# Token places computed by GpSimd at the start of the second attention instead of by VectorE at the end of the stage before it

## The reference, cut to what matters

```python
xn = _layernorm(x)
x = x + _L1_attn_ref(xn, ...) + _L1_ffn_ref(xn, ...)      # layer 1
# in _L1_ffn_ref:
scores = sigmoid(xf @ gate_w + bias)                       # (4096, 8)
top_scores, top_idx = top_k(scores, 2)
top_scores = top_scores / (sum(top_scores) + 1e-06)
w = zeros((T, E)).at[arange(T)[:, None], top_idx].add(top_scores)
...
combined = einsum('teh,te->th', eo * 0.1, w)
```

## Time and profile before

| | us |
|---|---|
| median of 3 runs | 1206.17 |
| lowest, highest | 1204.74, 1207.23 |
| the profiled execution | 1203.1 |
| its span, first to last instruction | 1201.4 |

### The profile page before, as it was taken

How to read it: one execution, slowest core, us unless ns; L and a number is a source line. 1 busy time by engine, 2 the same in 40 slices (tenths; PEclk the granted TensorE clock), 3 DMA queues, 4 the chain that set the end, 5 groups by cost and what they waited for, 6 DMA issues and landing times. The chain is left out here.

```text
span 1201.4 us, 22310 instructions
## 1 busy us (share of the span) xinstructions
PE 1078.3 (90%) x7591; PEld 595.4 (50%) x7598; DVE 930.1 (77%) x1984; ACT 724.4 (60%) x1110; POOL 471.8 (39%) x809
## 2 busy tenths in 40 slices
PE   4767878999999999999999886999999879999997
PEld 2335664333334344333334464444444358888874
DVE  7979997878888888888887353788878546777776
ACT  3647641466666666666666553466666657778761
POOL 7101221133323333332554320476776712566630
PEclk9988997799999999999999887699999989999999
DMA  5322592011211222122101022222222263677452
GB/s 141 97 89 65 113 147 31 19 54 55 72 63 56 82 72 74 55 84 71 57 5 35 1 78 83 66 62 67 68 62 68 68 198 120 200 243 243 157 133 78
DMA packets 99953, 106.10 MB, mean 88 GB/s; under 512 B 21505, under 2 KB 77334, under 8 KB 99776
## 3 DMA queue, kind: packets, MB, share of 16 engines
q1 hardware_dynamic: 93904, 95.65, 29.8%
q0 software_dynamic: 4992, 8.48, 2.1%
q10 hardware_dynamic: 944, 0.54, 0.2%
HBM read 65.20 MB, written 38.45 MB: 86 GB/s over the span
## 5 line engine op out<-in xcount | busy, mean ns | idle before, releaser
L1256 ACT ACTIVATE a_probs<-a_pst 128x1024 f32<-128x1024 f32 (+4 forms) x544 | 411.9, 808 | 206.8 <-PE a_pst L1200 199.4
L1279 DVE TENSOR_REDUCE a_tops<-a_ps 128x1 f32<-128x512 f32 (+9 forms) x624 | 338.2, 589 | 71.1 <-PE a_ps L1154 68.8
L1098 POOL TENSOR_SCALAR_AFFINE_SELECT a_probs<-a_probs 128x256 f32<-128x256 f32 (+3 forms) x384 | 180.2, 481 | 331.2 <-ACT a_probs L1256 326.8
L1154 PE MATMUL a_ps<-kp,qp 96*128 96x256 bf16 (+10 forms) x2112 | 291.0, 253 | 8.8 <-PEq L1407 4.5
L1200 PE MATMUL a_pst<-qp,kp 98*128 98x512 bf16 (+4 forms) x1088 | 260.8, 332 | 17.7 <-ACT a_probs L1256 12.7
L1154 PEld LDWEIGHTS a_ps<-kp,qp 96*128 96x128 bf16 (+1 forms) x2112 | 140.2, 99 | 214.2 <-DVE a_tops L1279 100.9
L1219 PE MATMUL a_po<-a_probs,vh 128*32 128x512 f32 (+4 forms) x2176 | 229.6, 498 | 12.1 <-POOL a_probs L1098 11.3
L1279 DVE TENSOR_REDUCE a_tops_lead<-a_ps 128x1 f32<-128x512 f32 x256 | 165.1, 685 | 19.1 <-PE a_ps L1154 18.3
L1200 PEld LDWEIGHTS a_pst<-qp,kp 98*128 98x128 bf16 (+1 forms) x1088 | 83.4, 99 | 113.5 <-ACT a_probs L1256 64.8
L1911 POOL DMA_INDIRECT chosen_rows<-e_slot_y,e_slot_x x92 | 93.3, 1014 | 96.9 <-DVE e_slot_y L2131 75.1
L2119 DVE TENSOR_TENSOR e_tails<-e_hidden,e_heads 128x512 fp32r<-128x512 f32 x124 | 86.0, 694 | 39.8 <-ACT e_heads L2053 37.6
(11 more groups left out here) (330 smaller groups left out, 1513.2 us busy)
## 6 DMA issues: line engine op xcount, KB each, us to landing
e_slot_w<-weight_parts SPq DMA_DIRECT2D x23, 1024.0 KB
qp<-q_parts SPq DMA_DIRECT2D x64, 96.0 KB
slot_rows<-empty_row SPq DMA_DIRECT2D x4, 1495.0 KB, 26.6
e_slot_x<-slot_rows SPq DMA_DIRECT2D x23, 260.0 KB, 3.2
a_raw<-in_wraw SPq DMA_DIRECT2D x18, 256.0 KB, 3.9
weight_parts<-first_rows SPq DMA_DIRECT2D x9, 512.0 KB, 4.4
weight_parts<-a_cut SPq DMA_DIRECT2D x9, 512.0 KB, 3.0
qp<-q_parts SPq DMA_DIRECT2D x64, 64.0 KB
```

What stands on the lines that cost most here:

```text
L1098: pool.affine_select(out=seen, in_=seen, compare_op=ALU.is_ge, fill=0.0, base=m0, pattern=[[0, 2], [1, mw]], channel_multiplier=-1 if laye ...
L1154: last = pe.matmul(bank[:, i * room + at:i * room + to], sb["qp"][slot][0:rows, j, f["qt"] * P:(f["qt"] + 1) * P], sb["kp"][slot][0:rows, ...
L1256: act.activation(probs[local % RING][0:st["rows"], 2 * part:2 * part + 2, st["off"]:CHUNK], p_st[part][0:st["rows"], :, st["off"]:CHUNK], ...
L1279: dve.tensor_reduce(out, scores, AX.X, ALU.max).then_inc(s["banks_read"], 1)
```

## The change

VectorE keeps three instructions at the end of `between_layers`: the totals are rounded as before, now into a tensor `counted` that stays, and the 256 columns of ranks are copied out of PSUM into a new tensor `ranks`. The rest is computed by GpSimd in the block of attention 1, behind `stage(0)` and `stage(1)` and before its first mask. GpSimd's version adds in three halving steps where VectorE had one `tensor_reduce`, and makes `passed_by` in eight instructions. Temporary tensors move from one block's memory to the other's.

```diff
@@ between_layers, VectorE
-            def place_tokens():
...
+            def copy_ranks():
+
                 dve.wait_ge(plan["ranked"], START + 1)
...
+                dve.tensor_scalar(sb["counted"][:, :], p_y[:, TILES * EXPERTS:(TILES + 1) * EXPERTS], float(CHUNK - 1), None, ALU.add)\
+                    .then_inc(plan["plan_steps"], 1)
+                dve.tensor_copy(sb["ranks"][:, :], p_y[:, 0:TILES * EXPERTS]).then_inc(plan["plan_steps"], 1)
+                dve.wait_ge(plan["plan_steps"], START + 1)
+                dve.tensor_scalar(sb["counted"][:, :], sb["counted"][:, :], (1 << 31) - CHUNK, None, ALU.bitwise_and)\
+                    .then_inc(plan["plan_steps"], 1)
...
-            place_tokens()
+            copy_ranks()
@@ attention, GpSimd
+            def place_tokens():
+
+                step = plan["plan_steps"]
+                ranks = sb["ranks"][:, :].rearrange("p (t e) -> p t e", e=EXPERTS)
+                narrow = [P, EXPERTS, EXPERTS]
+                pool.wait_ge(step, START + 3)
+                pool.tensor_copy(spread[:, :], sb["counted"][:, :]).then_inc(step, 1)
+                pool.wait_ge(step, START + 4)
+                pool.tensor_tensor(upto[:, :, :], sb["upto"][:, :, :], spread[:, :].unsqueeze(1).broadcast_to(narrow),
+                                   ALU.mult).then_inc(step, 1)
+                for i, half in enumerate((4, 2, 1)):
+                    pool.wait_ge(step, START + 5 + i)
+                    pool.tensor_tensor(upto[:, :, 0:half], upto[:, :, 0:half], upto[:, :, half:2 * half], ALU.add)\
+                        .then_inc(step, 1)
...
+                for i in range(EXPERTS):
+                    pool.tensor_scalar(passed_by[:, :, i], sb["firsts"][:, :], region_ends[:, i:i + 1], 1.0,
+                                       ALU.is_ge, ALU.mult).then_inc(step, 1)
...
+                for i, half in enumerate((4, 2, 1)):
+                    pool.wait_ge(step, START + EXPERTS + 12 + 2 * i)
+                    pool.tensor_tensor(chosen[:, :, :, 0:half], chosen[:, :, :, 0:half], chosen[:, :, :, half:2 * half],
+                                       ALU.add).then_inc(step, 1)
...
             stage(0)
             stage(1)
+            if layer == 1:
+                place_tokens()
             for what, n, k, part in order:
```

More of the change, by code:

```diff
@@ L962, in attention @@
         e = sb["counts"]["experts"]
+        if layer == 1:
+            plan = sb["counts"]["plan"]
+            spread = tmp("spread", [P, EXPERTS])
+            upto, region_base = tmp("upto", [P, EXPERTS, EXPERTS]), tmp("base", [P, EXPERTS])
+            place, chosen = tmp("place", [P, TILES, EXPERTS]), tmp("chosen", [P, TOPK, TILES, EXPERTS])
+            passed_by = tmp("passed_by", [P, SLOT_TILES, EXPERTS])
         if layer == 0:
@@ L1073, in draw_after @@
                                    channel_multiplier=-1).then_inc(drawn, 1)
+            def place_tokens():
[11 more added lines that the diff above has]
+                        .then_inc(step, 1)
+                region_ends = upto[:, :, 0]
+                pool.wait_ge(step, START + 8)
+                pool.tensor_tensor(region_base[:, :], region_ends, spread[:, :], ALU.subtract).then_inc(step, 1)
+                for i in range(EXPERTS):
+                    pool.tensor_scalar(passed_by[:, :, i], sb["firsts"][:, :], region_ends[:, i:i + 1], 1.0,
+                                       ALU.is_ge, ALU.mult).then_inc(step, 1)
+                pool.wait_ge(step, START + 9)
+                pool.tensor_tensor(place[:, :, :], ranks, region_base[:, :].unsqueeze(1).broadcast_to([P, TILES, EXPERTS]),
+                                   ALU.add).then_inc(step, 1)
+                pool.wait_ge(step, START + EXPERTS + 10)
+                for i in range(TOPK):
+                    pool.tensor_tensor(chosen[:, i, :, :], sb["hot"][:, i, :, :], place[:, :, :], ALU.mult).then_inc(step, 1)
+                for i, half in enumerate((4, 2, 1)):
+                    pool.wait_ge(step, START + EXPERTS + 12 + 2 * i)
+                    pool.tensor_tensor(chosen[:, :, :, 0:half], chosen[:, :, :, 0:half], chosen[:, :, :, half:2 * half],
+                                       ALU.add).then_inc(step, 1)
+                    pool.tensor_tensor(passed_by[:, :, 0:half], passed_by[:, :, 0:half], passed_by[:, :, half:2 * half],
+                                       ALU.add).then_inc(step, 1)
+                pool.wait_ge(step, START + EXPERTS + 18)
+                pool.tensor_copy(sb["slots"][:, :, :], chosen[:, :, :, 0]).then_inc(step, 1)
+                pool.tensor_scalar(sb["expert_of"][:, :], passed_by[:, :, 0], 1.0, float(EXPERTS - 1), ALU.mult, ALU.min)\
+                    .then_inc(step, 1)
@@ L1421, in between_layers @@
         den = tmp("den", [P, BT])
[L1422 to L1426, removed]
         p_t, p_y, p_xn, p_c, p_k, p_v = (bank(n) for n in "pt py pxn pc pk pv".split())
@@ L1732, in choose @@
                                   den[:, :].unsqueeze(2).broadcast_to([P, BT, TOPK]), ALU.mult).then_inc(step, 1)
-            def place_tokens():
[L1736 to L1739, removed]
-                dve.wait_ge(plan["ranked"], START + 1)
[L1741 to L1767, removed]
@@ L2206, in build @@
         keep("gates", [P, TILES, TOPK])
+        keep("ranks", [P, TILES * EXPERTS])
+        keep("counted", [P, EXPERTS], I32)
         keep("slots", [P, TOPK, TILES], U32)
```

## The result

| | before | with the change |
|---|---|---|
| median (us) | 1207.23 of 5 | 1200.74 of 5 |
| lowest, highest | 1204.74, 1208.61 | 1200.22, 1202.74 |
| the profiled execution | 1203.1 | 1200.41 |
| its span | 1201.4 | 1198.7 |

The ratio is 0.9956, 95% interval 0.9944 to 0.9968: 5.3 us faster, 3.9 to 6.8. (The kernel before ran again beside the changed one, so its median is now 1207.23. The ratio and its interval are an estimate of their own and not the quotient of the two medians, which differ by 6.5 us.) The forecast was 3.1 us less and 1203.1; the time lies in the range, and the gain is larger than the working gave.

What follows compares the result with a forecast made beforehand. VectorE's list at the end of `between_layers` was taken to hold up every engine: -3.43 us for shortening it and +0.3 for the collision make -3.1, so 1206.17 becomes 1203.1 us, range 1200.0 to 1205.6.

Steps and rivals of the forecast that it cites:

- What bounds the place: End of `between_layers`: every engine waits 4 us for VectorE's list of small instructions; VectorE still reports last after the change.
- The 3.43 us: End of `between_layers`: VectorE's list ends at 744.83 against 748.26, and all of this comes off attention 1's start.
- the rounding: Last of VectorE's three kept instructions, taken to follow the copy of the ranks, 0.17 us.
- TensorE's idle time: Before attention 1: about 1.0 us in place of 4.45, with nothing taken for it in the sum.
- idle time ahead of the experts: Sign of a wrong prediction: the 3.4 us return as idle time of all engines before the experts.
- GpSimd's chain: Start of attention 1: 25 instructions and twelve waits, 8.5 us, costing nothing on the path, 5.3 us to spare.
- The collision: First unit's tail in attention 1: L1293 on VectorE slowed beside GpSimd's chain, 0 to 0.88 us, taken as 0.3 lost.
- The clock: Start of attention 1: rival that TensorE keeps 2.4 GHz, giving 1199.9 us, chance 0.09; expected instead to fall after 5 to 8.
- The rival of a long chain: Start of attention 1: GpSimd's chain delays the masks, 25.5 us giving 1214.5; slower case, chance 0.06.
- The sum: Whole kernel: -3.43 + 0.3 = -3.1 us, taken off the median of 1206.17.
- The case to which the prediction gave 0.66: Whole kernel: the forecast case, 2.4 to 4.5 us faster.

Runs made afterwards that it cites:

- r4: The changed kernel with ten more copies of the ranks on VectorE at the end of `between_layers`; 0.9979 of the kernel before, 1198.84 us.
- r7: The changed kernel with GpSimd's chain cut in two, the second part waiting for the first unit's tail on VectorE; 0.9957 of the kernel before, 1201.36 us.
- r8: The changed kernel with nine more dependent additions of 256 columns on GpSimd behind the chain; 0.9973 of the kernel before, 1204.26 us.
- r1: The kernel before, without any edit, measured against itself; 1.0005, 1202.60 us.
- r3: The kernel before with unused tensors `ranks` and `counted` (1056 bytes) behind `gates`, no instruction changed; 0.9983 of the kernel before, 1199.66 us.

## Why the prediction was right, and where it wasn't

*What bounds the place.* Right. VectorE's list set the end of the block, and it still does, by 0.6 us (0.7 forecast). r4 lengthened it by 3.3 us and the release moved by 3.31.

*The 3.43 us.* Measured 3.52. The copy took 0.41 (0.42 forecast). What was off is the rounding: it was put behind the copy, and started 0.33 after the copy's start, since it doesn't depend on it. The forecast of TensorE's idle time, about 1.0, stands against 0.93. Nor did the time come back as idle time ahead of the experts: from the end of ScalarE's last copy in attention 1 (`a_o_raw`) to the release it is 4.12 us in both traces.

*GpSimd's chain.* It took 10.2 us against 8.5, so 4.1 us were to spare and not 5.3. The term that was mis-sized is the instruction with few columns: eight compares of 23 columns with an operand of one column took 3.04, 0.38 each, where 0.24 was taken from a copy of 64 columns; and two inputs of 256 took 0.71 in place of 0.63. Nothing came of it, since the chain lies under the wait for the first exponentials, as forecast. The chain takes 2.5 times VectorE's 4.10. The Trainium skill (GPSIMD Engine Reference, Engine selection) has a factor of about 2 for two inputs; here 0.71 against the 0.42 of L1757 is 1.7.

*The collision.* Right in kind and place, shown by r7. The size was 0.3 and is 0.44. It had been looked for in L1293 alone (now L1338), which went from 0.19 to 0.31, 0.12 more. The larger part is in the instruction before it, L1336: 0.51 where r7 has 0.18.

*The clock.* The rival that it holds didn't come: TensorE was idle 0.93 and not 4.45, and the clock fell all the same, 3.8 us in (5 to 8 forecast), and returned at the same distance from the stage's start. The Trainium skill (TensorE: Matmul & The Clock Gate, HAM oscillation) puts such a fall down to idle gaps between bursts. The long pause as that gap is not borne out here: without it the clock fell too. Counted from the first rank matmul, TensorE's last work before the stage, the fall even came at nearly the same distance: 4.5 to 7.1 us in the six traces with the work as before, 5.6 to 7.5 in the seven with the short list. The short gaps inside the stage were not varied.

*The rival of a long chain.* It said that masks are late from 13.8 us of chain and the kernel slower from 17.2. r8's chain is 17.4 us (743.28 to 760.69). Its masks are late by 3.1, and the trace terms, -0.6, put it near no change, as forecast. The time, 3.3 us under before, doesn't bear that out; it is lower by the remainder that all these kernels have.

*The sum.* -3.1 was forecast, and the trace terms are -3.1: 3.52 less 0.44. The measured gain is 4.5 to 6.4 in five comparisons. The step that fell short is the one that took the trace terms for the whole difference of the medians: 1.4 to 3.3 us more were gained than they give, and which part of that is the clock, the layout or chance isn't settled. That the time, 1200.74, still lies in the range is in part luck. The case to which the prediction gave 0.66 was 2.4 to 4.5 us; 5.3 lies beyond it, though the interval reaches down to 3.9. The range went as low as 1200.0 for the sake of the rival in which the clock holds (1199.9 by its own sum), and that didn't happen.

## What to carry to other kernels

A list of small dependent instructions on one engine at the end of a block is worth its whole length once it is last to report, and it can go to a slow engine if that engine has a wait longer than the chain right behind the block; here 10 us of GpSimd replaced 3.5 us of VectorE under a wait of 14. Look then at which VectorE instructions that read SBUF fall beside the chain, since these pay for it, and cut the chain there if they are on the path. And before a difference of 0.2% is explained, measure the kernel before against itself with an edit that does nothing: two such kernels (r1 and r3) had medians 3 us apart here, each with an interval of 1 us about its ratio. Nor is a whole stage of one profile held against that of another, where one kernel's own stage moves by 6 us.

## What the runs showed of the hardware

- An instruction on VectorE with one input in SBUF (128x32, f32 to bf16) took 0.51 beside GpSimd's chain and 0.18 without it (r7). It was expected only of the one with two inputs, which took 0.31 and 0.19.
- On GpSimd a compare of 23 columns with an operand of one column took 0.38; a multiply of 64 columns with a broadcast input took 0.32.
- VectorE's copies of 256 columns out of PSUM follow each other at 0.34 (ten in 3.39, r4), though one alone lasts 0.41.
- TensorE's clock fell to 1.2 GHz 3.8 us into a stage that it entered after 0.93 us of idle time.
- One stage of one program, attention 1, took 221.9, 226.9 and 228.3 us in three executions at whole times within 0.5%.
